# First stage of a state-space, normalisation and routing kernel: gate bias seeded in PSUM by ScalarE, one PSUM bank for each half of x's transposes, output rows in two pairs

## The chip, the cores and the metric

One Trainium2 chip, one core. The metric is the time of one execution on the device in microseconds, the median over runs. Before the change it is 476.87 us (three runs, 476.1 to 477.67).

## What is computed

The input x has 2 sequences of 4096 tokens with 256 features. The stage that is changed computes a small linear recurrence with a gate, a residual and a layer norm:

```python
a  = tanh(x @ WA.T);  b = x @ WB.T               # 16 states
h_t = a_t * h_{t-1} + b_t                        # scan over the sequence
g  = sigmoid(x @ Wg.T + bg)                      # gate, 256 features
dx = x @ WD.T + bD
y  = (h @ WC.T) * g + dx * (1 - g)
x1 = layernorm(x + y)
```

The second part, which the change leaves as it is, scores x1 with a router, picks 512 of the 4096 tokens of each sequence, runs attention and a feed-forward network on them, and writes them back normalised over rows that the first stage already wrote.

## The kernel before

The first stage runs over 16 groups of 512 tokens (G = 0 to 15, four token tiles of 128 each, so each group has two halves q = 0, 1). Every engine has its own instruction queue, executed in order; semaphores order them against each other. All loops over G are written out by hand, with work of several groups in flight. In one turn G the queues hold, in this order:

- **TensorE**: `transposes(G+2, 0)` (four 128x128 transposes of the first feature half of x, line 707), `gates(G, 0)`, `transposes(G+2, 1)`, `recurrence_inputs(G+1)` (lines 718 to 720), `gates(G, 1)`. A `gates` is `gate_inputs` (lines 731 to 733: for each of two token tiles six matmuls 512 wide, gate columns and dx columns side by side in one PSUM bank) and `state_products` (line 743: two matmuls 512 wide that add the state term -h @ WC.T to the dx columns and the biases to both; line 750: two 256 wide, h @ WC.T alone, into bank 7). Values are split into a high and a low part, so that each product is three matmuls.
- **ScalarE**: `normalise(G-2)` (line 1232, four rows of output), `copy_xT(G+2, 0)` (line 1203, high part of x transposed), `gate(G, 0)` (line 1215, sigmoid), `copy_xT(G+2, 1)`, `decays(G+1)` (line 1209, tanh), `round_h(G+1)` (line 1224), `gate(G, 1)`.
- **VectorE**: `products(G-1, 1)` (line 1466: state term plus x; line 1471: u = (g - 1) * dx'), `half_statistics(G-1, 0)` (lines 1483 and 1485: mean and variance, and the dot product with the router's weights), `rest_of_x(G+2, 0)` (line 1446, low part of x), `statistics(G-1)` (the second half's lines 1483 and 1485, then lines 1495 to 1500), `products(G, 0)`, `rest_of_x(G+2, 1)`, `scan(G+1)` (line 1459). Small steps of the router's selection stand between these from G = 9 on.
- **GpSimd**: `total(G-1, 1)` (line 519: s = s - u, both in SBUF), `scales(G-1)` (lines 533, 537 and 528: reciprocal roots), `total(G, 0)` (line 519), `rest_of_h(G+1)` (line 578: low part of the state). One turn each has `positions()`, `factors(0)` or `split_values(0)` before `rest_of_h`.
- **SyncE** loads x four groups ahead and stores a finished group (lines 457 and 459).

PSUM bank 0 holds the transposes of both feature halves, one after the other: `transposes(G+2, 1)` waits for `rest_of_x(G+2, 0)`. Bank 1 holds a copy of the router's weights (line 1583) and the means and variances of line 1495, so line 1485 reads one operand from SBUF (s) and one from PSUM. Banks 3 to 6 hold the gate and dx columns of the four token tiles. The sigmoid waits for `state_products` (semaphore `gd_done`).

Of the kernel before, what the change touches and what calls it, by code (L numbers as in the profile page):

```python
# [87 lines left out]
def build(nc, x_in, WA, WB, WC, WD, bD, Wg, bg, mask_in, pos_in, router_w, router_b,  # L88
          wq, wk, wv, wo, w1, w2, ln1, ln2, out):
    with ExitStack() as ctx:  # L90
# [45 lines left out]
        rb_col = sb("rb_col", [P, 1])  # L136
        minus_half = sb("minus_half", [P, NT])
# [18 lines left out]
        junk = arena2[:, 7168:8192].rearrange("p (t d) -> p t d", t=T)  # L156
        zero_state = sb("zero_state", [HROWS, 1])
# [113 lines left out]
        router_loaded = sem("router_loaded")  # L271
        gain_ready = sem("gain_ready")
# [18 lines left out]
        kept_ready = sems("kept_ready")  # L291
# [23 lines left out]
        sin_ready = sems("sin_ready")  # L315
# [41 lines left out]
        h_lo_ready = sem("h_lo_ready")  # L357
        gd_done = sem("gd_done")
# [20 lines left out]
        AGGR, CNT, BEL, TOT, PICK = 256, 272, 336, 400, 272  # L379
# [48 lines left out]
        def _(sp):  # L428
# [42 lines left out]
        def _(pool):  # L471
# [160 lines left out]
            def kept(b):  # L632
                pool.wait_ge(angle_ready[b], 1)
                for c in range(C):
                    pool.wait_ge(x_sel_in[b][c], 16)
                    pool.tensor_scalar(keep[b][:, c, :], x_sel[b][:, c, :], wf_sel[:, b, c, 1:2], keep_m[:, b, c:c + 1],
                                       ALU.mult, ALU.mult).then_inc(kept_ready[b], 1)
# [54 lines left out]
        def _(pe):  # L692
# [30 lines left out]
            def gate_inputs(G, q):  # L723
                if G > 0:
                    pe.wait_ge(u_ready, 2 * (G - 1) + q + 1)
                for t in range(2):
                    tt = 2 * q + t
                    for c in range(KD):
# [3 lines left out]
                        pe.matmul(o, hi, wgd_lo[:, c, :], start=False, stop=False)  # L732
                        pe.matmul(o, lo, wgd_hi[:, c, :], start=False, stop=False)  # L733

            def state_products(G, q):
# [4 lines left out]
                pe.wait_ge(h_lo_ready, G + 1)  # L740
                for t in range(2):
                    tt = 2 * q + t
                    mm = pe.matmul(ps[:, 3 + 2 * q + t, :], h_parts[j][:, tt * P:(tt + 1) * P], wc_d[:, :],  # L743
                                   start=False, stop=True)
# [440 lines left out]
        def _(act):  # L1185
# [13 lines left out]
            def copy_xT(G, c):  # L1199
# [3 lines left out]
                act.copy(x_hi[G % XS][:, c, :], ps[:, 0, :]).then_inc(x_hi_ready[c], 1)  # L1203
# [7 lines left out]
            def gate(G, q):  # L1211
                act.wait_ge(gd_done, 2 * G + q + 1)
                if G > 0:
                    act.wait_ge(u_ready, 2 * (G - 1) + q + 1)
                act.activation(g_sb[q][:, :, :], ps[:, 3 + 2 * q:5 + 2 * q, 0:D],  # L1215
                               ACT.Sigmoid).then_inc(g_ready, 1)
# [9 lines left out]
            def normalise(G):  # L1226
# [4 lines left out]
                for t in range(T):  # L1231
                    last = act.activation(ob_sb[G % 2][:, t, :], s_sb[G % 2][:, t, :], ACT.Identity,  # L1232
                                          bias=nb[G % 2][:, t:t + 1], scale=rq[:, b, n.start + t:n.start + t + 1])
                last.then_inc(ob_ready, 1)
# [78 lines left out]
            def sines(b):  # L1313
                act.wait_ge(angle_ready[b], 1)
                act.activation(trig[b][:, 4, :, :], trig[b][:, 3, :, :], ACT.Sin)
                act.activation(trig[b][:, 5, :, :], trig[b][:, 3, :, :], ACT.Sin, scale=0.5).then_inc(sin_ready[b], 1)
# [117 lines left out]
        def _(dve):  # L1434
# [7 lines left out]
            def rest_of_x(G, c):  # L1442
# [3 lines left out]
                dve.tensor_tensor(x_lo[G % XS][:, c, :], ps[:, 0, :], x_hi[G % XS][:, c, :].bitcast(F32),  # L1446
# [541 lines left out]
```

## Time and profile before

| what | value |
|---|---|
| median of three runs | 476.87 us |
| the profiled execution, its own time | 477.91 us |
| its span, first to last instruction | 475.8 us |
| first stage within the span | 0 to about 174 us |
| busy: TensorE, VectorE, ScalarE, GpSimd | 438.7, 394.8, 287.6, 182.0 us |
| mean granted TensorE clock | 0.987 of full speed |

A busy time is a share of the whole span, over stages with different limits. Rows of the timeline give a start, a duration, the engine, the line of the kernel, the operation, output and inputs; in square brackets stands how long the engine had been idle and whose signal ended that. PE is TensorE, DVE VectorE, ACT ScalarE, POOL GpSimd. Starts and durations are microseconds; in the view of one line the durations are nanoseconds (minimum/median/maximum). Durations of successive instructions on one engine overlap, so that the pitch from start to start is what one costs.

### The profile page before, as it was taken

How to read it: one execution, taken by the hardware profiler on the slowest of the kernel's cores; microseconds unless marked ns; L12 is line 12 of the kernel's file. 1: busy time of each engine (PE TensorE's matmuls, PEld its weight loads, DVE VectorE, ACT ScalarE, POOL GpSimd, SP SyncE). 2: the span in 40 equal slices, each digit the busy share in tenths (PEclk: the TensorE clock that was granted, in tenths of full speed). 3: DMA queues.
4: the chain of work that ended last, by engine and by line, in shares of the span. 5: the costliest groups of instructions: out<-in, count | busy, mean ns of one | idle time of the engine just before them, and what ended most of it. 6: DMA issues, size and time to landing. Idle time of an engine off the chain costs nothing.

```text
span 475.8 us, 10265 instructions
## 1 busy us (share of the span) xinstructions
PE 438.7 (92%) x3525; PEld 331.7 (70%) x3525; DVE 394.8 (83%) x1227; ACT 287.6 (60%) x617; POOL 182.0 (38%) x231
## 2 busy tenths in 40 slices
PE   8798999999999987899998999998998899999893
PEld 5587888777777753476775677677797577677692
DVE  4777899788998888986779999997966999996663
ACT  3435655465554626022767999995534999995640
POOL 8346757777577744066137000002000600000374
PEclk9899999999999999998999999999999999999997
DMA  7813244223441121026983000000000000000011
GB/s 242 260 45 92 88 135 132 88 90 93 131 132 47 44 89 45 1 68 218 328 273 90 2 2 3 1 3 1 1 0 1 2 2 2 3 2 1 1 40 49
DMA packets 29371, 33.89 MB, mean 71 GB/s; under 512 B 5861, under 2 KB 24969, under 8 KB 29321
## 3 DMA queue, kind: packets, MB, share of 16 engines
q1 hardware_dynamic: 23088, 24.78, 15.9%
q0 software_dynamic: 3520, 8.40, 5.8%
q8 instruction: 28, 0.46, 0.4%
q10 hardware_dynamic: 2712, 0.06, 0.3%
q14 instruction: 23, 0.18, 0.1%
HBM read 19.59 MB, written 13.63 MB: 70 GB/s over the span
## 4 chain that ended last, share of the span: by engine, by line
PE 35%; DVE 17%; issue 8%; POOL 6%; ACT 4%; DVEq 0%; POOLq 0%; ACTq 0%
DVE arena L1827 5%; PE ps L1011 5%; DVE big L422 4%; PE ps L1080 3%; PE ps L1028 3%; PE ps L1115 3%; PE ps L928 3%; PE ps L698 3%; PE ps L960 2%; PE ps L832 2%; PE ps L995 2%; POOL arena L519 2%; PE ps L885 1%; PE ps L1086 1%; PE ps L933 1%
## 5 line engine op out<-in xcount | busy, mean ns | idle before, releaser
L1350 ACT ACTIVATE arena<-arena,nmax 128x511 f32<-128x511 f32 x128 | 91.7, 719 | 3.6 <-DVE nmax L1827 3.4
L1827 DVE CUSTOM_DVE_ANT_0 arena<-ps,nmask 128x511 f32<-128x511 f32 x128 | 84.8, 683 | 0.6 <-issue 0.6
L1011 PE MATMUL ps<-ident,arena 128*128 128x128 f32 x512 | 78.6, 276 | 5.2 <-ACT big L422 2.3
L1011 PEld LDWEIGHTS ps<-ident,arena 128*128 128x128 f32 x512 | 58.5, 140 | 29.6 <-ACT arena L1350 18.0
L731 PE MATMUL ps<-wgd_hi,x_hi 128*128 128x512 f32 x128 | 51.6, 403 | 0.0
L733 PE MATMUL ps<-wgd_hi,x_lo 128*128 128x512 f32 x128 | 50.5, 394 | 0.0
L732 PE MATMUL ps<-wgd_lo,x_hi 128*128 128x512 f32 x128 | 50.3, 393 | 0.0
L995 PE MATMUL ps<-arena 96*128 96x512 bf16 x128 | 48.2, 383 | 0.8 <-DVE x_sel L1892 0.5
L422 DVE COPY big<-ps 128x512 f32<-128x512 f32 x64 | 43.9, 686 | 3.2 <-PE ps L1011 3.2
L519 POOL TENSOR_TENSOR arena<-arena 128x512 f32<-128x512 f32 x30 | 38.8, 1292 | 9.6 <-DVE arena L1471 7.9
L422 ACT COPY big<-ps 128x512 f32<-128x512 f32 x64 | 36.9, 577 | 3.2 <-PE ps L1011 1.6
L1232 ACT ACTIVATE ob_sb<-arena,nb,rq 128x256 f32<-128x256 f32 x64 | 33.1, 590 | 8.2 <-POOL nb L537 8.1
L1224 ACT CAST h_parts<-arena 48x512 fp32r<-48x512 f32 x16 | 9.9, 621 | 37.4 <-DVE arena L1459 37.4
L1446 DVE TENSOR_TENSOR x_lo<-ps,x_hi 128x512 fp32r<-128x512 f32 x32 | 21.9, 686 | 10.6 <-ACT x_hi L1203 10.6
L528 POOL TENSOR_TENSOR r<-v,minus_half 128x8 f32<-128x8 f32 x16 | 26.7, 1671 | 7.7 <-DVE v L1500 7.7
L533 POOL TENSOR_TENSOR rq<-vq,minus_half 128x4 f32<-128x4 f32 x16 | 16.2, 1011 | 35.3 <-DVE v L1500 35.3
L698 PE MATMUL ps<-ones_b 128*128 128x512 bf16 x106 | 27.0, 379 | 2.7 <-DVE arena L1466 1.5
L1215 ACT ACTIVATE arena<-ps 128x512 f32<-128x512 f32 x32 | 19.1, 598 | 16.3 <-PE ps L743 14.3
L1466 DVE TENSOR_TENSOR arena<-ps,arena 128x512 f32<-128x512 f32 x32 | 21.9, 683 | 8.0 <-PE ps L750 7.9
L733 PEld LDWEIGHTS ps<-wgd_hi,x_lo 128*128 128x128 f32 x128 | 24.0, 188 | 5.7
L731 PEld LDWEIGHTS ps<-wgd_hi,x_hi 128*128 128x128 f32 x128 | 24.2, 189 | 5.0
L732 PEld LDWEIGHTS ps<-wgd_lo,x_hi 128*128 128x128 f32 x128 | 24.1, 188 | 5.0
(267 smaller groups left out, 1029.9 us busy)
## 6 DMA issues: line engine op xcount, KB each, us to landing
arena<-in_L_attn_x SPq DMA_DIRECT2D x16, 512.0 KB, 4.6
out<-ob_sb SPq DMA_DIRECT2D x16, 512.0 KB, 3.1
w_sb<-in_L_ffn_w SPq DMA_DIRECT2D x2, 1024.0 KB, 11.5
mt_scratch<-nmask SPq DMA_DIRECT2D x8, 256.0 KB, 6.1
mt_scratch<-big SPq DMA_DIRECT2D x8, 256.0 KB
big<-in_L_attn_Wg SPq DMA_DIRECT2D x1, 256.0 KB, 4.2
big<-in_L_attn_WD SPq DMA_DIRECT2D x1, 256.0 KB, 4.8
wqk<-in_L_ffn_wq SPq DMA_DIRECT2D x1, 256.0 KB, 8.2
```

Of the source, the lines that this page charges most:

```text
L422: copy(prT[c % 2][:, h, :, :], ps[:, 2 + u % 2, :].rearrange("p (k n) -> p k n", k=C)).then_inc(prT_copied[u % 2], 1)
L519: pool.tensor_tensor(s, s, u_sb[q][:, :, :], ALU.subtract).then_inc(s_ready, 1)
L528: pool.tensor_tensor(r2[:, :, b, n], v2[:, :, b, n], minus_half[:, 0:2 * T].rearrange("p (k t) -> p k t", k=2), ALU.pow).then_inc(r2_ready, 1)
L698: pe.matmul(ps[:, bank, :], ones_b[:, :], ones_wide, start=True, stop=True)
L731: pe.matmul(o, hi, wgd_hi[:, c, :], start=(c == 0), stop=False)
L732: pe.matmul(o, hi, wgd_lo[:, c, :], start=False, stop=False)
L733: pe.matmul(o, lo, wgd_hi[:, c, :], start=False, stop=False)
L995: pe.matmul(ps[:, S_BANKS[b][u % AHEAD], :], qkT[0][:, hg * HG + h:hg * HG + h + 1, c * P:(c + 1) * P], qkT[1][:, hg * HG + h:hg * HG + h ...
L1011: mm = pe.transpose(ps[:, 2 + u % 2, k * P:(k + 1) * P], pr[u % 4][:, k * P:(k + 1) * P], ident[:, :])
L1232: last = act.activation(ob_sb[G % 2][:, t, :], s_sb[G % 2][:, t, :], ACT.Identity, bias=nb[G % 2][:, t:t + 1], scale=rq[:, b, n.start + t: ...
L1350: act.activation(pr[u % 4][:, 0:K - 1], sm[u % 4][:, 0:K - 1], ACT.Exp, bias=nmax[:, c, h:h + 1], scale=-1.0, accum_out=rsum[:, c, h:h + 1 ...
L1827: dve.tensor_tensor_reduce(sm[u % 4][:, 0:K - 1], ps[:, S_BANKS[b][u % AHEAD], 0:K - 1], nmask[b][:, c, 0:K - 1], 1.0, 3.4e38, ALU.add, AL ...
```

## The change

1. `transposes(G, c)` writes bank c, not bank 0, and waits for `rest_of_x(G-1, c)` alone. `copy_xT` and `rest_of_x` read bank c.
2. Bank 1 is thereby taken: the router's weights stay in SBUF (`rw_row`), and the means and variances go to SBUF (`mv1`). Line 1485 reads both operands from SBUF.
3. The gate columns of two token tiles share bank 3 + 2q, the dx columns bank 4 + 2q. Each 512-wide matmul of `gate_inputs` becomes two of 256, each with a weight load of its own.
4. From G = 1 on the gate's bias is not multiplied in: ScalarE copies a row of bg (`bg_row`, one more 128 KB load) into the bank after each sigmoid (`seed`), and the matmuls add to it. `state_products` then needs its first product for the dx columns alone: 256 wide.
5. The sigmoid waits for the gate's matmuls (`g_done`), VectorE's line 1471 now for `gd_done`.
6. ScalarE issues the four output rows as two pairs with `copy_xT(G+2, 0)` between.
7. Some pairs of semaphores become one, with counts to match.

```diff
@@ sync
+            sp.dma_start(bg_row[:, :, :], bg.rearrange("(a o d) -> a o d", a=1, o=1).broadcast_to((P, 1, D))).then_inc(router_loaded, 16)
@@ tensor
             def transposes(G, c):
-                if c == 0 and G > 0:
-                    pe.wait_ge(x_lo_ready[1], G)
-                elif c == 1:
-                    pe.wait_ge(x_lo_ready[0], G + 1)
+                if G > 0:
+                    pe.wait_ge(x_lo_ready[c], G)
                 for t in range(T):
-                    mm = pe.transpose(ps[:, 0, t * P:(t + 1) * P],
+                    mm = pe.transpose(ps[:, c, t * P:(t + 1) * P],
             def gate_inputs(G, q):
                 if G > 0:
+                    pe.wait_ge(g_seeded, 2 * (G - 1) + q + 1)
                     pe.wait_ge(u_ready, 2 * (G - 1) + q + 1)
-                        o = ps[:, 3 + 2 * q + t, :]
-                        pe.matmul(o, hi, wgd_hi[:, c, :], start=(c == 0), stop=False)
...
+                        pe.matmul(o[0], hi, wgd_hi[:, c, 0:D], start=(new and G == 0), stop=False, skip_group_check=True)
+                        pe.matmul(o[1], hi, wgd_hi[:, c, D:2 * D], start=new, stop=False, skip_group_check=True)
...
+                if G > 0:
+                    mm.then_inc(g_done, 1)
             def state_products(G, q):
-                    mm = pe.matmul(ps[:, 3 + 2 * q + t, :], h_parts[j][:, tt * P:(tt + 1) * P], wc_d[:, :],
+                    mm = pe.matmul(ps[:, 4 + 2 * q, t * D:(t + 1) * D], h_parts[j][:, tt * P:(tt + 1) * P], wc_d[:, D:2 * D],
@@ scalar
             def gate(G, q):
-                act.wait_ge(gd_done, 2 * G + q + 1)
+                act.wait_ge(g_done, 2 * G + q + 1)
+            def seed(G, q):
+                act.wait_ge(g_ready, 2 * G + q + 1)
+                act.copy(ps[:, 3 + 2 * q, :].rearrange("p (t d) -> p t d", t=2),
+                         bg_row[:, :, :].broadcast_to((P, 2, D))).then_inc(g_seeded, 1)
             for G in range(NGB + 2):
                 if G >= 2:
-                    normalise(G - 2)
+                    normalise(G - 2, 0)
                 if G + 2 < NGB:
                     copy_xT(G + 2, 0)
+                if G >= 2:
+                    normalise(G - 2, 1)
...
                     decays(G + 1)
+                    seed(G, 0)
                     round_h(G + 1)
...
                     gate(G, 1)
+                if G + 1 < NGB:
+                    seed(G, 1)
@@ vector
             def products(G, q):
                 dve.wait_ge(g_ready, 2 * G + q + 1)
+                dve.wait_ge(gd_done, 2 * G + q + 1)
             def half_statistics(G, q):
-                    step.done(dve.tensor_tensor_reduce(junk[:, t, :], s_sb[j][:, t, :], ps[:, 1, 0:D], 1.0, 0.0,
+                    step.done(dve.tensor_tensor_reduce(junk[:, t, :], s_sb[j][:, t, :], rw_row[:, :], 1.0, 0.0,
             def statistics(G):
-                mv = ps[:, 1, AGGR + 2 * T * j:AGGR + 2 * T * (j + 1)].rearrange("p (t m) -> p t m", t=T)
+                mv = mv1[j]
-            dve.wait_ge(router_loaded, 32)
-            dve.tensor_copy(ps[:, 1, 0:D], rw_row[:, :])
+            dve.wait_ge(router_loaded, 48)
```

## Rows read from the trace of the kernel before

**Rows 1.** Busy us by stretch: PE, PEld, DVE, ACT, POOL (instructions), PEclk, DMA share, GB/s.
```profile
52.00:62.00 10.00, 9.98 (x50) 8.18 (x49) 8.82 (x36) 5.57 (x11) 6.64 (x6) 1.00 0.39 116
```

**Rows 2.** Timeline of VectorE: line 1466 that follows line 1500, around four equal turns.
```profile
43.23 0.68 DVE L1466 TENSOR_TENSOR arena<-ps,arena 128x512 f32<-128x512 f32 x1
...
81.01 0.68 DVE L1466 TENSOR_TENSOR arena<-ps,arena 128x512 f32<-128x512 f32 x1
```

**Rows 3.** Timeline of TensorE: half a turn, and a wait for a free bank.
```profile
52.74 0.39 PE L731 MATMUL ps<-wgd_hi,x_hi 128*128 128x512 f32 x1
...
55.53 0.63 PE L743 MATMUL ps<-wc_d,h_parts 128*128 128x512 f32 x2
...
56.23 0.60 PE L707 MATMUL ps<-ident,arena 128*128 128x128 f32 x4
...
99.77 0.63 PE L707 MATMUL ps<-ident,arena 128*128 128x128 f32 x4 [0.88 <-DVE x_lo L1446]
```

**Rows 4.** Chain that ended last (start, us, what), last stage: 16 matmuls 256 wide.
```profile
456.20 1.91 PE ps L1106 x16
```

**Rows 5.** Chain that ended last, 153 to 167 us.
```profile
156.27 1.30 POOL h_parts L578
...
157.69 1.29 POOL arena L519
158.99 2.20 issue
```

**Rows 6.** Timeline of VectorE and ScalarE in the turn from 151.83 us.
```profile
151.83 0.68 DVE L1466 TENSOR_TENSOR arena<-ps,arena 128x512 f32<-128x512 f32 x1
...
154.92 0.62 ACT L1224 CAST h_parts<-arena 48x512 fp32r<-48x512 f32 x1 [2.51 <-DVE arena L1459]
...
156.20 0.69 DVE L1471 SCALAR_TENSOR_TENSOR arena<-arena,ps 128x512 f32<-128x512 f32 x1 [0.20 <-ACT arena L1215]
...
157.47 0.40 DVE L1485 CUSTOM_DVE_ANT_0 arena<-arena,ps 128x256 f32<-128x256 f32 x1
...
157.79 0.42 DVE L1485 CUSTOM_DVE_ANT_0 arena<-arena,ps 128x256 f32<-128x256 f32 x1
...
159.02 0.75 DVE L1483 BATCH_NORM_STATS2 stats<-arena 128x6 f32<-128x256 f32 x2 [0.80 <-POOL arena L519]
...
161.06 0.68 DVE L1466 TENSOR_TENSOR arena<-ps,arena 128x512 f32<-128x512 f32 x1
```

**Rows 7.** Single lines with the spread of their durations (ns, minimum/median/maximum).
```profile
L1485 DVE CUSTOM_DVE_ANT_0 arena<-arena,ps x64: 401/409/420, 28.9 to 177.8; 128x256 f32<-128x256 f32 x64
...
L1520 DVE TENSOR_SCALAR x_sel<-x_sel x8: 168/174/1289, 138.6 to 183.1; 128x32 int32<-128x32 int32 x8
...
L1531 DVE TENSOR_TENSOR arena<-x_sel,v_sb x16: 399/408/597, 174.1 to 202.5; 128x480 bf16<-128x480 bf16 x16
...
L528 POOL TENSOR_TENSOR r<-v,minus_half x16: 1637/1642/2102, 33.6 to 179.0; 128x8 f32<-128x8 f32 x16
```

**Rows 8.** Timeline of VectorE and GpSimd where those maxima lie.
```profile
138.63 1.46 DVE L1520 TENSOR_SCALAR x_sel<-x_sel 128x32 int32<-128x32 int32 x3
138.76 1.29 POOL L519 TENSOR_TENSOR arena<-arena 128x512 f32<-128x512 f32 x1
...
171.61 0.69 DVE L1476 TENSOR_TENSOR arena<-arena 128x512 f32<-128x512 f32 x1
171.70 2.10 POOL L528 TENSOR_TENSOR r<-v,minus_half 128x8 f32<-128x8 f32 x1
...
183.86 0.37 POOL L571 TENSOR_TENSOR x_sel<-x_sel,v_sb 128x96 f32<-128x96 f32 x1
183.90 0.60 DVE L1531 TENSOR_TENSOR arena<-x_sel,v_sb 128x480 bf16<-128x480 bf16 x1
```

**Rows 9.** Timeline at the start of the stage.
```profile
21.02 0.59 ACT L1203 CAST x_hi<-ps 128x512 fp32r<-128x512 f32 x1
...
24.16 1.27 DVE L1459 TENSOR_TENSOR_SCAN arena<-arena,ps 48x512 f32<-48x512 f32 x1 [1.83 <-ACT arena L1209]
```

More of the change, by code:

```diff
@@ L136, in build @@
         rb_col = sb("rb_col", [P, 1])
+        bg_row = sb("bg_row", [P, 1, D])
         minus_half = sb("minus_half", [P, NT])
@@ L156, in build @@
         junk = arena2[:, 7168:8192].rearrange("p (t d) -> p t d", t=T)
+        mv1 = [sb(f"mv1_{j}", [P, T, 2]) for j in range(2)]
         zero_state = sb("zero_state", [HROWS, 1])
@@ L357, in build @@
         h_lo_ready = sem("h_lo_ready")
+        g_done = sem("g_done")
         gd_done = sem("gd_done")
@@ L727, in gate_inputs @@
                     tt = 2 * q + t
+                    o = [ps[:, 3 + 2 * q + n, t * D:(t + 1) * D] for n in range(2)]
                     for c in range(KD):
                         hi, lo = (x[G % XS][:, c, tt * P:(tt + 1) * P] for x in (x_hi, x_lo))
-                        o = ps[:, 3 + 2 * q + t, :]
-                        pe.matmul(o, hi, wgd_hi[:, c, :], start=(c == 0), stop=False)
-                        pe.matmul(o, hi, wgd_lo[:, c, :], start=False, stop=False)
-                        pe.matmul(o, lo, wgd_hi[:, c, :], start=False, stop=False)
+                        new = t == 0 and c == 0
+                        pe.matmul(o[0], hi, wgd_hi[:, c, 0:D], start=(new and G == 0), stop=False, skip_group_check=True)
+                        pe.matmul(o[1], hi, wgd_hi[:, c, D:2 * D], start=new, stop=False, skip_group_check=True)
+                        pe.matmul(o[0], hi, wgd_lo[:, c, 0:D], start=False, stop=False, skip_group_check=True)
+                        pe.matmul(o[1], hi, wgd_lo[:, c, D:2 * D], start=False, stop=False, skip_group_check=True)
+                        mm = pe.matmul(o[0], lo, wgd_hi[:, c, 0:D], start=False, stop=(c == KD - 1), skip_group_check=True)
+                        pe.matmul(o[1], lo, wgd_hi[:, c, D:2 * D], start=False, stop=False, skip_group_check=True)
+                if G > 0:
+                    mm.then_inc(g_done, 1)
             def state_products(G, q):
@@ L740, in state_products @@
                 pe.wait_ge(h_lo_ready, G + 1)
+                if G == 0:
+                    for t in range(2):
+                        tt = 2 * q + t
+                        mm = pe.matmul(ps[:, 3 + 2 * q, t * D:(t + 1) * D], h_parts[j][:, tt * P:(tt + 1) * P], wc_d[:, 0:D],
+                                       start=False, stop=True, skip_group_check=True)
+                    mm.then_inc(g_done, 1)
                 for t in range(2):
                     tt = 2 * q + t
-                    mm = pe.matmul(ps[:, 3 + 2 * q + t, :], h_parts[j][:, tt * P:(tt + 1) * P], wc_d[:, :],
-                                   start=False, stop=True)
+                    mm = pe.matmul(ps[:, 4 + 2 * q, t * D:(t + 1) * D], h_parts[j][:, tt * P:(tt + 1) * P], wc_d[:, D:2 * D],
+                                   start=False, stop=True, skip_group_check=True)
                 mm.then_inc(gd_done, 1)
@@ L1202, in copy_xT @@
                     act.wait_ge(rec_done, 2 * (G - XS) + 2)
-                act.copy(x_hi[G % XS][:, c, :], ps[:, 0, :]).then_inc(x_hi_ready[c], 1)
+                act.copy(x_hi[G % XS][:, c, :], ps[:, c, :]).then_inc(x_hi_ready[c], 1)
             def decays(G):
@@ L1224, in round_h, with normalise @@
                 act.copy(h_parts[G % 2][0:HROWS, :], h_sb[G % 2][:, :]).then_inc(h_hi_ready, 1)
-            def normalise(G):
+            def normalise(G, half):
                 b, n = tokens(G)
@@ L1230, in normalise @@
                     act.wait_ge(out_stored[G % 2], 16 * (G // 2))
-                for t in range(T):
+                for t in (2 * half, 2 * half + 1):
                     last = act.activation(ob_sb[G % 2][:, t, :], s_sb[G % 2][:, t, :], ACT.Identity,
                                           bias=nb[G % 2][:, t:t + 1], scale=rq[:, b, n.start + t:n.start + t + 1])
-                last.then_inc(ob_ready, 1)
+                if half == 1:
+                    last.then_inc(ob_ready, 1)
             def load_positions():
```

26 lines of the change are left out of this document (15 added, 11 removed).

## The prediction

> **What bounds the kernel now.** I read the busy times by stretch first: in ten microseconds of the first stage TensorE is busy 9.98 at full granted clock, VectorE 8.82, GpSimd 6.64, ScalarE 5.57 [rows 1]. Busy shares don't say which engine sets the pace, so I then measured one turn of the loop on the timeline, from one line 1466 that follows line 1500 (call that moment v) to the next. Four turns run from 43.23 to 81.01 us, 9.445 us each [rows 2]; a late turn, without transposes to make, takes 161.06 - 151.83 = 9.23 us [rows 6]. The two figures have different causes.
>
> *TensorE's turn.* Twelve matmuls of `gate_inputs` take 55.53 - 52.74 = 2.79 us, the four state products 0.70 us [rows 3]; that comes twice a turn, beside the recurrence and the transposes. What is left of 9.445 us as idle is mostly a wait of the second transposes for `rest_of_x`, because both halves of x share bank 0; in one turn it is 0.88 us [rows 3].
>
> *GpSimd's ring.* Late in the stage the chain of waits is one ring: line 578, line 519 for the second half, 2.20 us in which VectorE does that half's statistics, then the roots, line 519 for the first half, and line 578 again [rows 5]. It is 9.23 us long and nothing in it depends on TensorE. So TensorE sets 9.445 us now, and 9.23 us stands right below it. A change that frees TensorE can win 0.2 us a turn and no more, unless it shortens this ring too.
>
> **The change part by part.** *TensorE.* Per turn 24 matmuls 512 wide become 48 of 256, and four of the state products 512 wide become 256. Sixteen matmuls 256 wide, each with its own weight load, take 1.91 us, 0.119 each [rows 4]; a 512-wide one costs 2.79 / 12 = 0.2325. Gates: 48 x 0.119 - 24 x 0.2325 = +0.13 us. State products: 4 x (0.119 - 0.2325) = -0.45 us. Even with all its waits kept TensorE's turn falls to 9.445 - 0.32 = 9.12 us, and the bank for each half takes some of these waits away. Either way it is under the ring's 9.23, which hides what is uncertain here.
>
> *ScalarE.* Two seeds a turn. The trace has no copy from SBUF to PSUM; the nearest rows are 0.62 us (SBUF to SBUF, at 154.92) and 0.59 (PSUM to SBUF, at 21.02) [rows 6, 9]. Two make 1.2 us on an engine that is busy 5.57 of 10 [rows 1]. The first follows `decays`, well before `round_h` can start; the second stands ahead of two output rows and `copy_xT`. The pairing takes two rows off the path to that copy, which about cancels the second seed. `rest_of_x` waits for the copy, and VectorE doesn't come to it earlier than computed below: I price the seeds at nothing; with that cover gone it would be 0.6 us a turn. The sigmoid's earlier release is worth nothing either: on ScalarE it stands behind `round_h`, which waits for the scan [rows 6]. `bg_row` goes ahead of loads of x that are used a good while after they land, and means and variances in SBUF keep their small instructions: both zero, within 0.1 us a turn either way.
>
> *Line 1485 with both operands in SBUF.* On this part the sign hangs. Today it reads the router's weights from PSUM, and its 64 executions all last 401 to 420 ns [rows 7], although the second one at 157.79 runs beside GpSimd's line 519 [rows 5, 6]. VectorE's instructions that work from SBUF to SBUF fare otherwise. Line 1520 has a median of 174 ns and once took 1289, at 138.7 us, just while GpSimd ran line 519 (138.76 to 140.05): held up 1.1 us, until about 0.1 us before that ended. Line 1531, two SBUF inputs, once took 597 ns instead of 408, beside line 571. And the other way round: GpSimd's line 528 took 2102 ns instead of 1642 where VectorE's line 1476, two SBUF inputs, had started 0.09 us earlier [rows 7, 8]. The two engines share something that one instruction holds for nearly its whole length.
>
> Where would line 1485 meet GpSimd? Count from v in the turn of [rows 6]: `round_h` at +3.09 after the scan, the sigmoid behind it, line 1471 at +4.37, the first 1485 at +5.64, the second at +5.96. On GpSimd line 578 runs from +4.44 to +5.74, line 519 from +5.86 [rows 5]. All these offsets are fixed by chains that start at v, and the change alters none of them. Line 578 lets go about 0.1 us before its end, so the first 1485 passes. Line 519 comes at +5.86, is held until the first 1485 lets go (about +5.95, 0.1 us before its end) and then holds on until about +7.1. The second 1485 finds it taken, and VectorE is past it only at +7.4. `rest_of_x(G+2, 0)` behind it takes 0.6, so the second half's statistics start at +8.0 and not at 159.02 - 151.83 = +7.19. From there to the next v are 161.06 - 159.02 = 2.04 us [rows 6]: a turn of 10.05 us, +0.6 against 9.445. Queued behind the held 1485 are `rest_of_x` and the statistics, and for these GpSimd's roots wait: the ring itself has grown.
>
> No row shows a 1485 from SBUF, so its cost has two bounds: nothing (the turn is then the ring's 9.23 to 9.3 us, -0.17) or the full 1.29 us of line 519 with `rest_of_x` behind it (+0.9). I take +0.6, for it is nearest to what line 1520 lost to the same line 519.
>
> *Sum.* Nine turns at +0.61 (the four of [rows 2] and five later ones without extra GpSimd work): +5.5. The two last turns have no `rest_of_x`: statistics at +7.4, turn 9.44 against 9.23: +0.4. Three turns in which positions, split values or the issue of small loads hold GpSimd or ScalarE up anyway: 0.3 each for small collisions, +0.9. That is +6.8 us. *Start.* The scan of group 1 waits 1.83 us for `decays` [rows 9], which come behind the second transposes of group 2, and those behind `rest_of_x`. With its own bank that wait goes; what is late next is ScalarE's copy at 21.02, after which `decays` (0.6) could end at 22.2 and the scan start at 22.3: -1.9 us (bounds 0 and 24.16 - 21.02 = 3.1). Together +4.9 us. On the profiled execution (477.91 us, 1.04 over the median of the runs) that is 482.8; on the median, which I predict, 481.8 us.
>
> **The rivals.**
> (a) *The forecast*: line 519 goes ahead of the second 1485: 481.8 us, 479 to 486 with the bounds.
> (b) *VectorE keeps its hold over both 1485.* Line 519 then starts at about +6.27 and ends at +7.5; the turn is 9.6 us. Nine turns at +0.1, +0.8 for the last two, +0.6 for the three, -1.9 at the start: +0.4, 477.3 us, 475.5 to 479. For it: the second 1485 is issued within hundredths of the moment the first lets go. Against it: line 519 has waited since +5.86, and GpSimd did get in between the four 1520 [rows 8]. The Trainium skill has a rule on this, in "SBUF — State Buffer", section "Who interferes with whom": a VectorE instruction with two SBUF inputs contends with a GpSimd instruction that reads SBUF, the first to issue holds the shared ports for the whole instruction, and issue order decides who blocks. By that rule line 519 goes ahead of the second 1485, so it speaks for (a), 481.8, over (b), 477.3; no row here shows the order among a running, a waiting and a later instruction.
> (c) *Line 1485 meets nothing*, because this custom operation reads its second operand otherwise. This is the rival on the other side. The ring sets 9.27 us, not TensorE: five plain turns at -0.17, less from the others, in all -1.7, and -1.9 at the start: 473.3 us. It decides if the durations stay near 410 ns with both operands in SBUF. Against it stand three lines of different kinds that show the hold [rows 7].
> (d) *The narrow matmuls cost more than their columns.* With 56 of them TensorE's turn would pass 10 us from 9.12 + 56 x 0.016, that is 0.135 us each, on; 0.119 in a row of sixteen [rows 4] nearly excludes it.
>
> **How the numbers follow.** (a) 0.55, (b) 0.25, (c) 0.15, 0.05 for (d) and the unforeseen. The likeliest is (a), 481.8 us. A measurement of this kernel tells about 0.3% (1.4 us) from no change. Faster by more: nearly all of (c) and a fifth of (b), 0.20. Within: half of (b) and the low end of (a), 0.17. Slower: 0.63. The range goes from 475.5, which leaves out (c), to 486, the bound of (a) with +0.9 a turn.
>
> **What the profile will show.** Right: 1485's durations in two groups, with a quarter of them well over 1 us beside line 519, turns near 10.05 us, TensorE idle for other reasons than `rest_of_x`, the scan of group 1 near 22.3 us, the gate's matmuls 0.119 us apart. Wrong: 1485 at 410 ns throughout and turns near 9.25 (then (c)); line 519 lengthened to 1.6 us and turns near 9.6 (then (b)); or a turn set by ScalarE, with `rest_of_x` waiting for the copy.

## The result and the profile after

The changed kernel takes 484.42 us (median of four runs, 484.2 to 485.38) against 476.5 us for the kernel before beside it: a ratio of 1.0166, 95% interval 1.0142 to 1.019. It is slower by 7.9 us. The profiled execution of after took 484.2 us, with a span of 482.1 us.

In after the lines have moved: the dot products of line 1485 are line 1517, GpSimd's lines 519 and 578 are 524 and 583, `rest_of_x` is line 1476, the scan 1489, statistics 1515 and 1532, the first line of `products` 1496.

First VectorE's costliest lines in the first stage, 10 to 185 us (busy us and mean ns of one, then the idle time before them), and the spread of line 1517's durations (ns, minimum/median/maximum):

```profile
L1517 DVE CUSTOM_DVE_ANT_0 arena<-arena,rw_row 128x256 f32<-128x256 f32 x64 | 38.8, 642 | 0.0
L1515 DVE BATCH_NORM_STATS2 stats<-arena 128x6 f32<-128x256 f32 x64 | 23.8, 414 | 3.7 <-POOL arena L524 3.4 <-DVE Wf L1539 0.2
```
```profile
L1517 DVE CUSTOM_DVE_ANT_0 arena<-arena,rw_row x64: 399/415/1534, 25.6 to 182.9; 128x256 f32<-128x256 f32 x64
```

The median has hardly moved from [rows 7], the maximum has gone from 420 to 1534 ns: 13 of the 64 took over 1 us, and a median hides an instruction that is held one time in five. The mean of 642 ns shows it, 64 x (642 - 409) ns = 14.9 us of VectorE's time, 409 being the median in [rows 7]. Now one turn of after on the timeline, VectorE and GpSimd, to be laid beside [rows 6]; this turn runs from 92.61 to 102.65 us:

```profile
96.98 0.69 DVE L1502 SCALAR_TENSOR_TENSOR arena<-arena,ps 128x512 f32<-128x512 f32 x1 [0.73 <-ACT arena L1232]
97.08 1.29 POOL L583 TENSOR_TENSOR h_parts<-arena,h_parts 16x512 fp32r<-16x512 f32 x1
97.58 0.74 DVE L1515 BATCH_NORM_STATS2 stats<-arena 128x6 f32<-128x256 f32 x2
98.25 0.41 DVE L1517 CUSTOM_DVE_ANT_0 arena<-arena,rw_row 128x256 f32<-128x256 f32 x1
98.50 1.30 POOL L524 TENSOR_TENSOR arena<-arena 128x512 f32<-128x512 f32 x1
98.58 1.50 DVE L1517 CUSTOM_DVE_ANT_0 arena<-arena,rw_row 128x256 f32<-128x256 f32 x1
100.02 0.68 DVE L1476 TENSOR_TENSOR x_lo<-ps,x_hi 128x512 fp32r<-128x512 f32 x1
100.62 0.74 DVE L1515 BATCH_NORM_STATS2 stats<-arena 128x6 f32<-128x256 f32 x2
102.65 0.68 DVE L1496 TENSOR_TENSOR arena<-ps,arena 128x512 f32<-128x512 f32 x1
```

Line 583 ends at 98.37 and the first dot product passes. Line 524 starts at 98.50, while that is running; the second, at 98.58, takes 1.50 us. It gets through at 100.02, 0.22 us after line 524 has ended; `rest_of_x` and the statistics behind it are late, and the turn is 10.04 us instead of 9.445 [rows 2]. What line 524 has summed is ready at 99.80, but the statistics of that half stand behind the held dot product and `rest_of_x` and start at 100.62; GpSimd's roots wait for them, and so the ring of [rows 5] has grown. Line 1515, with one input from SBUF, is not held: its pair takes 0.74 us beside line 583 (97.58) as well as beside nothing (100.62).

Turns, from one start of the line that ends the statistics (1500, after: 1532) to the next, in us:

| turn | 1 | 2 to 5 | 6 | 7 | 8 | 9 | 10 | 11 | 12 | 13 | 14 | 15 |
|---|---|---|---|---|---|---|---|---|---|---|---|---|
| before | 11.04 | 9.44 to 9.45 | 11.13 | 9.44 | 9.95 | 10.03 | 9.67 | 10.90 | 9.70 | 9.23 | 9.24 | 8.59 |
| after | 11.34 | 10.04 to 10.06 | 11.43 | 10.04 | 10.76 | 11.05 | 10.26 | 11.09 | 10.63 | 9.46 | 9.40 | 8.60 |

That adds up to +7.5 us. The first of these starts comes 2.5 us earlier (29.59 instead of 32.12), the last 5.0 us later (183.83 instead of 178.82). The span is longer by 6.3 us; the medians differ by 7.9, because the profiled execution of before was itself 1.4 us over its median, and that of after 0.2 under its own.

### The profile page after: what moved, and what is told of

It is laid out like the page before. It is cut to its first block, busy times and chain, and to the rows that moved or that the text cites. A ratio compares the mean times of both kernels' runs of the same rounds, so it can differ in the third digit from the quotient of the medians.

```text
span 482.1 us, 11117 instructions
## 1 busy us (share of the span) xinstructions
PE 436.7 (91%) x3913; PEld 349.5 (72%) x3913; DVE 406.8 (84%) x1226; ACT 302.7 (63%) x647; POOL 183.5 (38%) x231
## 4 chain that ended last, share of the span: by engine, by line
PE 31%; DVE 22%; issue 8%; ACT 4%; POOL 3%; DMA 2%; DVEq 0%; POOLq 0%; ACTq 0%
DVE arena L1858 6%; PE ps L1027 5%; DVE big L426 4%; PE ps L1096 3%; PE ps L1044 3%; PE ps L1131 3%; PE ps L703 3%; PE ps L976 2%; PE ps L848 2%; PE ps L1011 2%; DMA arena<-in_L_ffn_attention_mask,row_m 2%; DVE arena L1517 2%; PE ps L1102 1%; PE ps L1122 1%; PE ps L983 1%
## 5 line engine op out<-in xcount | busy, mean ns | idle before, releaser
L1027 PE MATMUL ps<-ident,arena 128*128 128x128 f32 x512 | 78.7, 276 | 5.4 <-ACT big L426 2.3
L1256 ACT ACTIVATE ob_sb<-arena,nb,rq 128x256 f32<-128x256 f32 x64 | 34.5, 593 | 9.2 <-POOL nb L542 9.2
L1517 DVE CUSTOM_DVE_ANT_0 arena<-arena,rw_row 128x256 f32<-128x256 f32 x64 | 38.8, 642 | 0.0
L736 PE MATMUL ps<-wgd_hi,x_hi 128*128 128x256 f32 x128 | 37.4, 292 | 0.0
L740 PE MATMUL ps<-wgd_hi,x_lo 128*128 128x256 f32 x128 | 36.4, 285 | 0.0
L738 PE MATMUL ps<-wgd_lo,x_hi 128*128 128x256 f32 x128 | 36.2, 283 | 0.0
L741 PE MATMUL ps<-wgd_hi,x_lo 128*128 128x256 f32 x128 | 36.1, 282 | 0.0
L737 PE MATMUL ps<-wgd_hi,x_hi 128*128 128x256 f32 x128 | 36.1, 282 | 0.0
L739 PE MATMUL ps<-wgd_lo,x_hi 128*128 128x256 f32 x128 | 36.1, 282 | 0.0
L1502 DVE SCALAR_TENSOR_TENSOR arena<-arena,ps 128x512 f32<-128x512 f32 x32 | 21.8, 681 | 11.3 <-ACT arena L1232 11.2
L710 PE MATMUL ps<-ident,arena 128*128 128x128 f32 x128 | 20.9, 290 | 7.0 <-DMA arena<-in_L_attn_x 6.9
```

The costliest lines, as they stand in the source:

```text
L736: pe.matmul(o[0], hi, wgd_hi[:, c, 0:D], start=(new and G == 0), stop=False, skip_group_check=True)
L737: pe.matmul(o[1], hi, wgd_hi[:, c, D:2 * D], start=new, stop=False, skip_group_check=True)
L738: pe.matmul(o[0], hi, wgd_lo[:, c, 0:D], start=False, stop=False, skip_group_check=True)
L740: mm = pe.matmul(o[0], lo, wgd_hi[:, c, 0:D], start=False, stop=(c == KD - 1), skip_group_check=True)
L1027: mm = pe.transpose(ps[:, 2 + u % 2, k * P:(k + 1) * P], pr[u % 4][:, k * P:(k + 1) * P], ident[:, :])
L1517: step.done(dve.tensor_tensor_reduce(junk[:, t, :], s_sb[j][:, t, :], rw_row[:, :], 1.0, 0.0, ALU.mult, ALU.add, dots[:, b, n.start + t:n. ...
```

## Experiments

All kernels ran beside the kernel before on the same chip. A turn is counted as in the table above; a plain turn is one of turns 2 to 5, and a common turn is the value that most of the undisturbed ones take.

| kernel | median us | before beside it | ratio, 95% interval | plain turns us |
|---|---|---|---|---|
| before, row from SBUF | 486.48 | 477.45 | 1.0191 [1.0169, 1.0214] | 10.04 |
| before, two banks | 483.99 | 477.6 | 1.014 [1.0093, 1.0186] | 10.04 |
| after, one bank | 478.1 | 477.45 | 0.9998 [0.9972, 1.0024] | 9.18 to 10.31 |
| after, no dot products | 468.95 | 477.45 | 0.9818 [0.979, 0.9846] | 8.64 to 10.51 |
| after, dot products behind the statistics | 481.27 | 477.45 | 1.0084 [1.0061, 1.0107] | 9.97 |
| before, dot products behind the scan | 473.17 | 477.6 | 0.991 [0.9884, 0.9936] | 9.22 |
| one bank, dot products behind the scan | 472.59 | 477.6 | 0.9886 [0.9828, 0.9943] | 8.70 to 9.11 |
| after, dot products behind the scan | 489.65 | 477.6 | 1.0242 [1.0203, 1.0281] | 10.77 |
| before, two banks at the start | 475.5 | 477.53 | 0.996 [0.994, 0.998] | 9.44 |
| the same, dot products behind the scan | 469.2 | 477.53 | 0.982 [0.9786, 0.9854] | 9.22 |
| with seeds and narrow products as well | 467.66 | 477.53 | 0.9788 [0.9753, 0.9823] | 8.85 to 10.02 |
| and with loads ahead of stores | 466.17 | 477.38 | 0.9773 [0.9754, 0.9792] | 8.68 to 8.90 |

### Is it the operand?

*Before, row from SBUF.*

```diff
-   dve.tensor_tensor_reduce(junk[:, t, :], s_sb[j][:, t, :], ps[:, 1, 0:D], 1.0, 0.0, ...
+   dve.tensor_tensor_reduce(junk[:, t, :], s_sb[j][:, t, :], rw_row[:, :], 1.0, 0.0, ...
```

> The kernel before with one operand exchanged: the dot products of line 1485 read the router row from SBUF instead of PSUM, everything else as before. Theory (the two SBUF operands of line 1485 are held by GpSimd's line 519): the second instruction of the pair that meets line 519 takes 1.3 to 1.6 us instead of 0.41, turns rise from 9.445 to about 10.05 us, and as nothing of the change's gain at the start is there, the kernel comes out slower than the change itself, near 484 to 487 us. Rival (the loss of the change lies in seeds, narrow matmuls or the new waits): line 1485 stays near 0.41 us and the time within 1 us of 476.5.

One operand, and the kernel before is 9.0 us slower. The spread of its line 1485, and the pair that meets line 519 in the turn that begins near 93 us:

```profile
L1485 DVE CUSTOM_DVE_ANT_0 arena<-arena,rw_row x64: 400/414/1510, 26.3 to 183.1; 128x256 f32<-128x256 f32 x64
```
```profile
98.99 0.41 DVE L1485 CUSTOM_DVE_ANT_0 arena<-arena,rw_row 128x256 f32<-128x256 f32 x1
99.23 1.30 POOL L519 TENSOR_TENSOR arena<-arena 128x512 f32<-128x512 f32 x1
99.32 1.50 DVE L1485 CUSTOM_DVE_ANT_0 arena<-arena,rw_row 128x256 f32<-128x256 f32 x1
```

The same picture as in after, with wide products and no seeds. The plain turns are those of after to 0.02 us.

*Before, two banks.* The bank part alone: both halves of x in banks of their own, `rw_row` and `mv` in SBUF.

```diff
+   if G > 0: pe.wait_ge(x_lo_ready[c], G)
-   mm = pe.transpose(ps[:, 0, ...
+   mm = pe.transpose(ps[:, c, ...
-   ... s_sb[j][:, t, :], ps[:, 1, 0:D], 1.0, 0.0, ...
+   ... s_sb[j][:, t, :], rw_row[:, :], 1.0, 0.0, ...
```

> The kernel before with the bank part of the change alone: a bank for each half of x's transposes, router row and moments in SBUF; no seeds, no narrow products, no paired rows. Theory (the bank part brings the whole loss, by the operand place): turns of 10.04 us with a dot product of 1.5 us in each, as in the change, and 484 to 486.5 us; the scan of group 1 within 0.4 us of where it stands in the change. Rival (the change's loss needs seeds or narrow matmuls as well): turns under 9.7 us and a time under 480 us.

483.99 us, at the lower end of what was expected, with plain turns of 10.04 to 10.05. The bank part accounts for 6.4 of the change's 7.9 us, and its interval (1.0093 to 1.0186) takes in the change's whole ratio; what seeds, narrow products and paired rows add is not told apart from nothing.

*After, one bank.* The opposite: seeds, narrow products and paired rows stay, the bank part goes.

```diff
-   mm = pe.transpose(ps[:, c, ...
+   mm = pe.transpose(ps[:, 0, ...            # with the waits of before
-   ... s_sb[j][:, t, :], rw_row[:, :], 1.0, 0.0, ...
+   ... s_sb[j][:, t, :], ps[:, 1, 0:D], 1.0, 0.0, ...
```

> The changed kernel with its bank part undone: both halves of x's transposes go through bank 0 again with the old waits, the router row and the aggregated moments lie in PSUM bank 1 again; seeds, narrow products and ACT's rows two and two stay. Theory (operand place): line 1517 stays at 0.41 us everywhere, turns of 9.25 to 9.45 us, time 473 to 477 us. Rival (seeds, narrow matmuls or waits cost the time): turns stay near 10.0 us and the time at 482 us or more.

```profile
L1519 DVE CUSTOM_DVE_ANT_0 arena<-arena,ps x64: 401/410/421, 29.7 to 178.5; 128x256 f32<-128x256 f32 x64
```

No dot product is held and the loss is gone; the time is that of before, 0.9998. It misses the expected 473 to 477 us by a little: undisturbed turns take 9.2 us, a little under what was expected, but turn 2 takes 10.31, where TensorE, after a wait of 2.2 us, had a mean granted clock of 0.76 and 0.90 of full level (40 to 50 us), and turn 4 takes 9.77, where it waited 1.0 us for x to land; and the gain at the start went with the bank.

### What the dot product costs, and where it stands in the ring

*After, no dot products.*

```diff
-   for t in (2 * q, 2 * q + 1):
+   for t in ():
        step.done(dve.tensor_tensor_reduce(junk[:, t, :], ...
```

> The changed kernel without its 64 dot products (line 1517 is left out, the dots are zeros, so the selection of tokens differs). It prices the instruction by itself. Theory: the whole loss of the steady turns goes, turns are TensorE's, 9.25 to 9.4 us, and the time is 471 to 474.5 us, as with the dot products moved. Rival (seeds, narrow matmuls or transposes' waits cost the time): turns of 9.7 us or more remain.

468.95 us, 15 us under the change and 2 us under what was expected. The common turn is 8.84 us, the late ones 8.70: well under the 9.23 us that the prediction took as the floor that GpSimd's ring sets. (Turn 3 takes 10.51, after a wait of TensorE of 2.2 us for x to land.) The whole time is a rough measure here: with other tokens picked, the part behind the first stage isn't the same work. The turns don't depend on that.

*After, dot products behind the statistics.*

```diff
    dve.tensor_scalar(v2[:, 1, b, n], ...).then_inc(var_ready, 1)
+   half_dots(G, 0)
+   half_dots(G, 1)
```

> The changed kernel with the four dot products of a group (line 1517) issued behind the statistics of that group, when GpSimd takes its roots on narrow operands, instead of between the statistics; operands stay in SBUF. Theory (collision with line 524 in time): no dot product over 0.6 us in the steady turns, GpSimd's ring loses the 0.8 us of the second pair as well, TensorE sets turns of 9.25 to 9.4 us, time 471.5 to 475 us. Rival (two SBUF operands are slow beside anything GpSimd does, or the loss lies elsewhere): dot products stay over 1 us beside the roots or turns near 10 us, time 481 us or more.

Here my theory of the move fell. Not one dot product is held, and yet plain turns take 9.97 us and the kernel 481.27 us. VectorE in that kernel:

```profile
L1524 DVE CUSTOM_DVE_ANT_0 arena<-arena,rw_row x64: 407/419/424, 27.5 to 179.6; 128x256 f32<-128x256 f32 x64
```
```profile
68.86 0.16 DVE L1538 TENSOR_SCALAR v<-mv 128x4 f32<-128x4 f32 x1
68.94 0.42 DVE L1524 CUSTOM_DVE_ANT_0 arena<-arena,rw_row 128x256 f32<-128x256 f32 x1
...
69.97 0.42 DVE L1524 CUSTOM_DVE_ANT_0 arena<-arena,rw_row 128x256 f32<-128x256 f32 x1
70.32 0.68 DVE L1496 TENSOR_TENSOR arena<-ps,arena 128x512 f32<-128x512 f32 x1
...
72.12 1.26 DVE L1489 TENSOR_TENSOR_SCAN arena<-arena,ps 48x512 f32<-48x512 f32 x1
```

Behind the statistics VectorE does the four dot products (1.38 us), then the first half's products, `rest_of_x` and the scan; and the scan leads to `round_h`, line 583, line 524 for the second half and the statistics again. The ring therefore has a second branch that runs through VectorE from one end of statistics to the scan, and it is full. The late turns, in which `rest_of_x` drops out one half after the other, tell the shares. In turn 14, without it, four dot products behind the statistics make 8.84 us, against 8.70 with none and 9.24 with two between the halves' statistics. In turn 13, with one `rest_of_x` ahead of the scan, they make 9.44. In plain turns the other `rest_of_x` comes in too: it waits 0.77 us for ScalarE's copy, starts at 76.81, just before line 524 ends (76.84), and so puts the second half's statistics off by its own length, to 9.97.

*Behind the scan.* If so, the place for them is behind the scan, where VectorE idles until TensorE has made the second half's product (1.4 us in the kernel without dot products). Three kernels have this move: the kernel before, the one with one bank, and after. The dot products of the last group stay between its statistics.

```diff
    if G + 1 < NGB:
        scan(G + 1)
+   if 0 < G < NGB:
+       half_dots(G - 1, 0)
+       half_dots(G - 1, 1)
```

> The kernel before with the four dot products issued behind the next scan, nothing else; row in PSUM, wide products, one bank. It tells whether TensorE or GpSimd's ring sets 9.445 us. If TensorE sets it, as the prediction has it: turns stay at 9.35 to 9.45 us and the time within 1.5 us of 476.5. Rival (the ring through VectorE's dot products sets it): turns fall to 9.0 us or less, and the time to 472 us or less.

Between the two: plain turns of 9.22 us and 473.17 us. TensorE from 60 to 100 us, the kernel before first (PE's busy us and count stand first behind the length of the stretch, PEclk third from the end):

```profile
60.00:100.00 40.00, 38.31 (x189) 31.16 (x188) 33.83 (x111) 22.24 (x41) 28.15 (x31) 1.00 0.35 110
```
```profile
60.00:100.00 40.00, 39.48 (x195) 32.54 (x194) 35.27 (x119) 22.94 (x42) 29.43 (x32) 1.00 0.39 119
```

With the dot products out of the way TensorE is busy 39.48 of 40 us. Busy time alone doesn't prove that it sets the turn, for a short wait hides under the end of the matmul ahead of it: in the four plain turns of before TensorE counts as busy for 37.72 of 37.78 us. The starts show the wait. The last state products ahead of the second transposes, and these transposes, in before and then with the dot products moved:

```profile
59.90 0.40 PE L750 MATMUL ps<-wc_r,h_parts 128*128 128x256 f32 x2
60.32 0.63 PE L707 MATMUL ps<-ident,arena 128*128 128x128 f32 x4
```
```profile
59.19 0.40 PE L750 MATMUL ps<-wc_r,h_parts 128*128 128x256 f32 x2
59.43 0.60 PE L707 MATMUL ps<-ident,arena 128*128 128x128 f32 x4
```

From start to start that is 0.42 us in before and 0.24 after the move, alike in each of the four turns, and the other matmuls keep their distances to a few hundredths. So TensorE's work with wide products is 9.22 us a turn, and the 9.445 us of before was that work plus a wait of the second transposes for `rest_of_x`, which stands behind VectorE's dot products.

> The changed kernel with one bank and the router row in PSUM again, and the four dot products of a group issued behind the next scan, where VectorE idles until line 766's product. Theory (GpSimd's ring runs through VectorE's dot products, 0.70 us of it, and TensorE with narrow products needs 8.7 to 9.1 us): turns of 8.75 to 9.1 us, time 468 to 473 us. Rival (the ring of 9.23 us doesn't contain the dot products, or ScalarE sets the turn): turns stay at 9.2 us and the time at 475 us or more.

As expected: common turns of 8.86 us, 472.59 us. Seeds and narrow products take 0.36 us a turn off TensorE.

> The changed kernel (operands of the dot products in SBUF) with the four dot products issued behind the next scan, where GpSimd's line 524 and then line 583 run. Theory (two SBUF operands are held by GpSimd's operations on SBUF, and hold them): the first dot product of most turns lasts 1.0 to 1.6 us and line 583 or 524 is lengthened in some; part of it falls into idle time, so turns of 9.1 to 9.7 us, and 473 to 480 us, behind the same move with the row in PSUM by 3 us or more. Rival (the place in the order alone matters): both kernels with this move within 2 us of each other.

The same move with the row in SBUF costs 17 us more than with the row in PSUM: 489.65 us, plain turns of 10.77 us, well beyond what was expected. First the kernel with the row in PSUM, then this one:

```profile
63.19 1.30 POOL L524 TENSOR_TENSOR arena<-arena 128x512 f32<-128x512 f32 x1
63.28 0.39 DVE L1526 CUSTOM_DVE_ANT_0 arena<-arena,ps 128x256 f32<-128x256 f32 x1
63.60 0.41 DVE L1526 CUSTOM_DVE_ANT_0 arena<-arena,ps 128x256 f32<-128x256 f32 x1
63.94 0.41 DVE L1526 CUSTOM_DVE_ANT_0 arena<-arena,ps 128x256 f32<-128x256 f32 x1
64.28 0.41 DVE L1526 CUSTOM_DVE_ANT_0 arena<-arena,ps 128x256 f32<-128x256 f32 x1
```
```profile
63.11 0.40 DVE L1524 CUSTOM_DVE_ANT_0 arena<-arena,rw_row 128x256 f32<-128x256 f32 x1
63.14 1.52 POOL L524 TENSOR_TENSOR arena<-arena 128x512 f32<-128x512 f32 x1
63.43 1.51 DVE L1524 CUSTOM_DVE_ANT_0 arena<-arena,rw_row 128x256 f32<-128x256 f32 x1
64.80 1.27 POOL L583 TENSOR_TENSOR h_parts<-arena,h_parts 16x512 fp32r<-16x512 f32 x1
64.88 1.48 DVE L1524 CUSTOM_DVE_ANT_0 arena<-arena,rw_row 128x256 f32<-128x256 f32 x1
66.29 0.41 DVE L1524 CUSTOM_DVE_ANT_0 arena<-arena,rw_row 128x256 f32<-128x256 f32 x1
```

From PSUM four dot products run beside line 524 and none is held. From SBUF the two engines take turns: the first dot product lengthens line 524 by 0.22 us, line 524 holds the second, line 583 the third, and what takes 1.41 us from PSUM (63.28 to 64.69) takes 3.59 (63.11 to 66.70).

### The start of the stage

*Before, two banks at the start.* Each half has a bank of its own in the first three groups only; then bank 1 is free, and the router row is copied into it.

```diff
+   def x_bank(G, c): return c if G < 3 else 0
-   mm = pe.transpose(ps[:, 0, ...
+   mm = pe.transpose(ps[:, x_bank(G, c), ...
    if G + 1 < NGB: scan(G + 1)
+   if G == 0: step.link(dve.tensor_copy(ps[:, 1, 0:D], rw_row[:, :]))
```

> The kernel before with a bank for each half of x for the first three groups alone and the router row copied into PSUM after them; nothing else. It isolates what the bank part brings at the start, without the SBUF operand. Theory: 9.4 to 9.9 us between the first two scans instead of 11.43 with TensorE's granted clock at full level from 20 to 25 us, turns of 9.445 us as before, dot products of 0.41 us, 474 to 475.5 us. Rival (the start gain is given back, or was chance): 11.4 us between the scans, or 476.5 us.

As expected: 9.46 us between the first two scans, plain turns of 9.44, 2 us faster than before. The scans of the first two groups in before (the second is in [rows 9]), in this kernel, and in before with the row from SBUF:

```profile
12.73 1.27 DVE L1459 TENSOR_TENSOR_SCAN arena<-arena,zero_state,ps 48x512 f32<-48x512 f32 x1
```
```profile
11.77 1.27 DVE L1465 TENSOR_TENSOR_SCAN arena<-arena,zero_state,ps 48x512 f32<-48x512 f32 x1
21.23 1.26 DVE L1465 TENSOR_TENSOR_SCAN arena<-arena,ps 48x512 f32<-48x512 f32 x1
```
```profile
11.77 1.27 DVE L1459 TENSOR_TENSOR_SCAN arena<-arena,zero_state,ps 48x512 f32<-48x512 f32 x1
21.62 1.27 DVE L1459 TENSOR_TENSOR_SCAN arena<-arena,ps 48x512 f32<-48x512 f32 x1 [0.33 <-ACT arena L1209]
```

TensorE's busy time and granted clock from 15 to 25 us, in the order before, after, before with the row from SBUF:

```profile
15.00:20.00 5.00, 1.84 (x13) 1.34 (x12) 4.22 (x8) 2.13 (x3) 1.05 (x1) 0.99 1.05 353
20.00:25.00 5.00, 5.00 (x18) 4.11 (x19) 2.55 (x4) 2.11 (x4) 1.29 (x1) 0.67 0.38 84
```
```profile
15.00:20.00 5.00, 3.66 (x26) 3.19 (x25) 3.81 (x7) 2.54 (x4) 0.62 (x1) 1.00 1.07 368
20.00:25.00 5.00, 5.00 (x45) 5.00 (x44) 3.84 (x6) 3.96 (x8) 2.55 (x2) 1.00 0.38 73
```
```profile
15.00:20.00 5.00, 2.44 (x15) 2.09 (x16) 3.62 (x8) 2.74 (x5) 0.10 (x1) 1.00 1.08 343
20.00:25.00 5.00, 5.00 (x27) 4.17 (x26) 3.09 (x4) 2.35 (x5) 2.58 (x2) 1.00 0.20 41
```

In before TensorE idles, its clock falls to 1.2 GHz for part of the next stretch, and the recurrence's matmuls stand 0.43 us apart instead of 0.23. In all nine profiles with two banks at the start TensorE is busy 3.27 to 4.02 of the five microseconds from 15 to 20, its clock stays at 2.4 GHz up to 25 us, and 9.43 to 9.48 us lie between the first two scans. Of the five with one bank four lost the clock (0.50 to 0.67) and took 11.43 to 11.50 us. The fifth, with the row from SBUF, kept it: 9.85 us. So, by this one profile, of the start's 1.95 us the clock makes 1.58 and the wait itself 0.37. Why that one profile kept its clock, with TensorE busy 2.44 us where two others with 2.43 lost it, stays open; its other four runs took 486.42 to 486.97 us against 483.31 for the profiled one.

### Together

*Two banks at the start, dot products behind the scan* (those of the last two groups stay where they were), first with wide products and no seeds, then with the change's seeds and narrow products.

> The same two moves on the kernel before, with wide gate and state products and no seeds: a bank for each half in the first three groups, dot products behind the next scan. Against the kernel with seeds and narrow products it tells what these are worth once the dot products are off the ring. Theory (TensorE sets 9.23 us with wide and 8.85 us with narrow products): 470 to 472.5 us, 2 to 3 us over the kernel with narrow products. Rival (seeds and narrow products are worth nothing): the same time within 1 us.

> The changed kernel with a bank for each half of x for the first three groups alone, then one bank again and the router row copied into the PSUM bank that came free; four dot products behind the next scan, those of the last two groups between the statistics as before. Theory: seeds and narrow products bring turns of 8.85 us, two banks at the start bring 9.45 us between the first two scans instead of 11.5, and both add up: 468 to 470.5 us. Rival (what is won at the start or in the turns is given back behind the first stage): 472 us or more.

469.2 and 467.66 us, each a little under its expected range. Both beat both kernels, the second by 2.1% against before. Apart the two moves brought 2 us (the start) and 4.4 us (the dot products, 473.17 against 477.6), together 8.3. The surplus comes in part from the last two groups: turns 14 and 15 take 9.24 and 8.59 us here, 8.69 and 10.34 where the dot products of all groups but the last were moved. What seeds and narrow products are worth on top is less than the expected 2 to 3 us, 1.5 with overlapping intervals: their common turn is 8.85 us instead of 9.22, but turn 2 takes 9.97 and turn 4 10.02. Before the first of them TensorE waits 2.1 us for `rest_of_x` and its clock falls (0.81 of full level from 35 to 40 us, 0.85 in the next five); in the other it waits for x to land.

*Loads ahead of stores.* In after, too, the transposes wait for x itself. From 30 to 160 us (line waited for: us in total, times, longest):

```profile
PE ps L710 <- DMA arena<-in_L_attn_x: 6.9, 8, 1.7
PE ps L759 <- POOL h_parts L583: 4.9, 4, 1.9
```

The buffer of x is free at the end of a group's `products`, but SP issues the load into it only behind the store of the group before, which waits for the output rows. The last kernel turns the two round on SP's queue:

```diff
-   for G in range(NGB):
+   for G in range(NGB + 1):
        if G + XBUF < NGB: ...                  # the load, as it was
-       sp.wait_ge(ob_ready, G + 1); sp.dma_start(out_rows[G], ...)
+       if G > 0: sp.wait_ge(ob_ready, G); sp.dma_start(out_rows[G - 1], ...)
```

> The kernel with two banks at the start, dot products behind the scan, seeds and narrow products, and on SP the load of the next x issued ahead of the store of the group before instead of behind it. In that kernel TensorE waits 2.7 us in four places (30 to 140 us) for x to land, up to 1.1 us at once, and two plain turns take 9.97 and 10.02 us. Theory (these waits are the load's place behind the store): no wait of the transposes for x over 0.2 us, the fourth plain turn back at 8.85 us, 465 to 467 us. Rival (the load is late for its bandwidth or for the release of its buffer): the waits stay and the time within 0.7 us of 467.7.

466.17 us, 0.9773 of before, as expected. The runs overlap with those of the kernel without this move (467.66 us), but the waits show what it does: from 30 to 140 us TensorE no longer waits for the load, only for `rest_of_x` and once for line 587 (583 in after), and turn 4 takes 8.80 us instead of 10.02. TensorE is busy 39.41 of 40 us from 60 to 100, at full clock:

```profile
PE ps L719 <- DVE x_lo L1485: 3.7, 4, 2.1
PE ps L768 <- POOL h_parts L587: 0.4, 1, 0.4
```
```profile
60.00:100.00 40.00, 39.41 (x313) 38.16 (x312) 36.78 (x120) 29.16 (x55) 30.92 (x34) 1.00 0.33 107
```

## Why the prediction held, point by point

*Sign and mechanism: right.* The turn came out as it was counted. Offsets from v in the turn shown, with v at 92.61: the first dot product +5.64, line 524 +5.89 (forecast +5.86), the second past at +7.41 (+7.4), the second half's statistics +8.01 (+8.0), the turn 10.04 (10.05). The two kernels that change the operand and the bank alone show the cause. What the two engines share is not told apart further: only one place of the row in SBUF was tried. The Trainium skill, "SBUF — State Buffer", section "Who interferes with whom", has two SBUF inputs contend with a GpSimd instruction that reads SBUF; the trace agrees for the dot product too, with 1.50 us against 0.41, and with 0.41 throughout where one operand is in PSUM. Rivals (b) and (c) are out: line 524 is not at 1.6 us with turns of 9.6, and dot products don't stay at 410 ns. The order that no row of before showed is seen now: line 524, which starts while the first dot product runs, goes ahead of the second. Rival (d) is out as well: 23 narrow matmuls of the gates start between 84.39 and 86.98 us in after, 0.118 us apart.

*The sum: 2.6 us too small* (481.8 against 484.42). For the profiled execution 482.8 was forecast and 484.2 measured, 1.4 us more, from three terms:
- Nine turns at +0.61 (turns 2 to 5, 7 to 10 and 12 of the table). Six came to 0.59 to 0.61, the other three to 0.81, 1.02 and 0.93. In the turn of 1.02 two dot products are held, 0.92 us by line 583 at 119.05 and 1.49 us by line 524 at 119.91: where GpSimd is late with line 583, the first of the pair no longer passes. The prediction counted the later turns as plain ones. In all 0.9 us more than forecast. Turns 13 and 14 gave +0.39 (forecast +0.4), turns 1, 6 and 11 +0.79 (forecast +0.9).
- The start: -2.5 us instead of -1.9, 0.6 us the other way; 0.46 us of the 2.5 is the first scan, which was already that much earlier.
- Behind the first stage, where the code is the same, after takes 1.3 us more (298.27 us from the last start in the table of turns to the end of the span, against 296.98). Kernels with the statistics in the same place took 297.07 to 297.83, so part of it is the spread of that part. The chain of after waits in it for a gather of mask rows, TensorE for 0.8 us:

```profile
233.91 8.47 DMA arena<-in_L_ffn_attention_mask,row_m
```

 In before TensorE's own work ended last there. The last kernel above waits 1.1 us for this gather and takes 298.31 us; the one ahead of it, without loads ahead of stores, doesn't wait for it and takes 298.07. No run separates the gather from the spread.

The other 1.2 us lie in the step from the profile to the median. The prediction took 1.04 us off, because the profile of before stood that much over its median; that of after stood 0.2 us under its own.

*TensorE sets 9.445 us: half right.* Its work is 9.22 us with wide products. The rest was a wait of the second transposes for `rest_of_x`, as the prediction had it; that this wait comes from VectorE's dot products, and would go with them, it didn't see. The forecast of 0.32 us less with narrow products was good (0.36 measured, 9.22 to 8.86).

*The ring of 9.23 us as a floor: wrong as a floor.* The 2.20 us of statistics in [rows 5] contain two dot products that nothing on the ring needs. Without them a late turn takes 8.70 us. The prediction said that a change can win 0.2 us a turn unless it shortens the ring, and did not ask which work on the ring could leave it.

*The start: size right by luck, cause wrong.* The 1.83 us in [rows 9] were put down to the wait of the transposes. That wait was worth 0.37 in the one profile that kept its clock, and the rest were matmuls at half the clock. The row to read was the granted clock of that stretch, 0.67, which the prediction didn't. That the bank took both away, 1.95 us against the 1.9 forecast, is luck.

*Seeds at nothing: held as far as it can be told.* One seed takes 0.58 us, and the kernel with seeds and without the bank part stands at 0.9998 of before. `rest_of_x` waits for ScalarE's copy 1.1 us in the whole first stage of after, 5.7 us in before, so the sign of a turn set by ScalarE is missing.

*Not foreseen:* with the wait for `rest_of_x` gone the transposes wait for the load of x, 6.9 us in all. That costs nothing in the plain turns of after, which the ring sets (10.04 to 10.06 us). Once TensorE sets them it can cost a turn over a microsecond (10.02 instead of 8.85). After the longest of these waits, 1.7 us, the granted clock of after was 0.88 and 0.77 of full level from 40 to 50 us.

## What to carry to other kernels

Before an operand moves from PSUM to SBUF, list what GpSimd runs beside that instruction: the price is not in the instruction's own duration but in the line of GpSimd that it meets, and a move in the order may make it meet two. When a ring sets the pace, ask of each instruction on it whether anything on the ring needs its result; moving the dot products that were not needed brought 4.4 us, more than the change's seeds and narrow products (0.6 to 1.5 us on top of it) or its two banks at the start (2 us). A bank that is wanted for two uses can serve both, one after the other: two banks for the first three groups, then the router row.

## What was not expected of the hardware

- A custom VectorE reduction of two 128x256 operands, 0.41 us, takes 1.48 to 1.53 us from SBUF beside a GpSimd addition of 1.29 us, and lengthens that to 1.52 us when it is first. From PSUM it runs beside it in 0.39 to 0.42 us.
- GpSimd's root on 128x4 operands (line 538) doesn't hold it: beside it the dot products from SBUF took 0.42 us each, and the root 1.11 us instead of 1.01.
- Idle time of TensorE can cost twice: waits of 1.5 to 2.2 us were followed by a time at 1.2 GHz, in before at the start (mean 0.67 of full level from 20 to 25 us), and near 40 us in after (0.88, then 0.77) and with one bank (0.76, then 0.90). Not always: the last kernel's wait of 2.1 us was followed by 1.00, and so was the wait of 1.5 us at the start of before with the row from SBUF.
